# Third block's up product by Strassen's scheme (Winograd's form) over 1024 tokens

## The chip, the cores and the metric

One core of one Trainium2 chip runs the whole program. The metric is device time in microseconds (us); lower is better. The kernel is written instruction by instruction: each engine (PE the matmul engine, ACT, DVE and POOL the elementwise engines, SP the issuer of DMAs) runs its own list in order and meets the others by semaphores only.

## The reference, cut to what matters

`x` has 32 blocks of 128 tokens of 512 features, float32. Two transformer blocks run one after the other; the kernel computes them in three stages, A (attention with 16 heads and layer norm), B (attention with one head over each block of 128 tokens) and C (the MLP of the second transformer block). The change concerns C and what feeds it:

```python
h = film(rmsnorm(x, norm2_w), cond, film2_w, film2_b)      # (32, 128, 512)
h = jax.nn.gelu(h @ mlp_w1 + mlp_b1, approximate=False) @ mlp_w2 + mlp_b2
return x_in + h                                            # w1 512 x 2048, w2 2048 x 512
```

`h @ mlp_w1` is called the up product, the one with `mlp_w2` the down product.

## The kernel before, in words

Every float32 operand of a large product is split in a high half, rounded to fp32r, and a low half, the difference; a product of two such operands takes three matmuls (high with high, high with low, low with high), `split_product`, lines 625 to 627. The 32 blocks are worked in NG = 8 groups of 4 blocks (512 tokens).

Stage B (`body_b(g, first, last)` of every engine, unrolled over g = 0 to 7): PE does four projections of the group's input (`h_g`, m = 0 to 3), then for each block b values (`values_b`), scores, the transpose of the exponentials (`transpose_pb`, L984) and the product with the values (`attend_b`). The last block's transpose and product of a group come after `h_g` 0 and 1 of the next group. Beside it ACT, DVE and POOL prepare the next group: ACT squares and sums the rows (`squares_b`, L1196), DVE makes mean plus epsilon (L1560), POOL raises to the power -1/2 (L1920) and scales the block (`norm_b`, L1923), PE transposes it (L937), ACT applies scale and shift (`scale_b`, L1133) and rounds (L1257), DVE subtracts (L1368). On ACT, `squares_b(g+1, 2)` and `squares_b(g+1, 3)` stand ahead of the first `next_h` of group g, and so ahead of its first exponential (L1308). `xb` has two slots: SP issues a load of it (L486) when the block two earlier has been scaled by POOL. In B the weights of the MLP's first layer are also loaded, rounded by ACT and made low by DVE, one eighth for each group (`split_w1`, L1284), and stay in SBUF.

Stage C (`body_c(g, first, last)`, groups 1 to 6 in a loop of the hardware): PE runs 16 tiles f of 128 hidden features. `up(g, f)` is 12 matmuls of 128 x 512 into bank f % 2; ACT takes the gelu from that bank (L1345), DVE rounds and subtracts (L1847, L1368), and `down(g, f)` follows LAG = 3 tiles later with 12 matmuls into banks 2 to 5. Norms of the next group are spread between the tiles; its transposes (L1055) come near the group's end. DVE adds the residual from the banks (L1859), POOL having added the bias to it (L1905), and SP stores.

The order of everything is written out by hand; there is no planner.

## Time and profile before

| what | value |
|---|---|
| time, median of 3 runs | 1519.54 us (1518.88 to 1519.66) |
| profiled execution's own time | 1519.62 us |
| its span | 1517.8 us |
| PE busy | 1508.4 us (99%), 8904 matmuls |
| DVE / ACT / POOL busy | 826.9 / 588.5 / 586.8 us |
| granted TensorE clock | 1.0 |
| DMA | 125.28 MB, mean 83 GB/s |

The span is from the first to the last instruction of the profiled execution; what lies between it and that execution's time is start and end. PE is busy from end to end, the other engines about half of the time. Stage C begins at about 804.5 us of the span.

### The profile page before, as it was taken

How to read it: one execution, taken by the hardware profiler on the slowest of the kernel's cores; microseconds unless marked ns; L12 is line 12 of the kernel's file. 1: busy time of each engine (PE TensorE's matmuls, PEld its weight loads, DVE VectorE, ACT ScalarE, POOL GpSimd, SP SyncE). 2: the span in 40 equal slices, each digit the busy share in tenths (PEclk: the TensorE clock that was granted, in tenths of full speed). 3: DMA queues.
4: the chain of work that ended last, by engine and by line, in shares of the span. 5: the costliest groups of instructions: out<-in, count | busy, mean ns of one | idle time of the engine just before them, and what ended most of it. 6: DMA issues, size and time to landing. Idle time of an engine off the chain costs nothing.

```text
span 1517.8 us, 24576 instructions
## 1 busy us (share of the span) xinstructions
PE 1508.4 (99%) x8904; PEld 1231.2 (81%) x8904; DVE 826.9 (54%) x1723; ACT 588.5 (39%) x1877; POOL 586.8 (39%) x506
## 2 busy tenths in 40 slices
PE   8999999999999999999999999999999999999999
PEld 5888888888887668888888888888888888888887
DVE  6777777877866676677766242332425233242522
ACT  4655565655544445655554221211212122121210
POOL 6757666676645545545552212030211202121100
PEclk9999999999999999999999999999999999999999
DMA  7222222222126236544444020010201001020100
GB/s 252 67 97 72 90 86 80 96 74 94 56 85 214 93 126 201 165 150 161 152 126 150 31 70 15 33 51 0 76 7 69 14 27 56 0 76 7 56 0 28
DMA packets 64350, 125.28 MB, mean 83 GB/s; under 512 B 6848, under 2 KB 10944, under 8 KB 64256
## 3 DMA queue, kind: packets, MB, share of 16 engines
q1 hardware_dynamic: 63584, 123.95, 24.3%
q8 instruction: 55, 0.90, 0.2%
q14 instruction: 39, 0.32, 0.1%
q10 hardware_dynamic: 672, 0.10, 0.0%
HBM read 98.67 MB, written 25.36 MB: 82 GB/s over the span
## 4 chain that ended last, share of the span: by engine, by line
PE 97%; POOL 1%; DVE 1%; DMA 0%; issue 0%; SPq 0%; ACT 0%
PE bank L625 27%; PE bank L627 27%; PE bank L626 27%; PE bank L716 4%; PE bank L709 2%; PE bank L727 2%; PE bank L1030 2%; PE bank L937 1%; PE bank L766 1%; PE bank L758 1%; PE bank L1055 1%; PE bank L640 1%; POOL xa L1888 1%; DMA wgb<-wb_t_in 0%; POOL rstd L1885 0%; PE bank L650 0%
## 5 line engine op out<-in xcount | busy, mean ns | idle before, releaser
L1847 DVE CAST g_hi<-gf 128x512 fp32r<-128x512 f32 x128 | 68.7, 537 | 427.9 <-ACT gf L1345 427.9
L1345 ACT ACTIVATE gf<-bank,cols 128x512 f32<-128x512 f32 x128 | 88.3, 690 | 513.5 <-PE bank L627 513.5
L1170 ACT ACTIVATE pa<-bank,neg_max 128x128 f32<-128x128 f32 x512 | 181.7, 409 | 136.2 <-DVE neg_max L1463 136.2
L625 PE MATMUL bank<-w_hi,g_hi 128*128 128x512 f32 x512 | 200.5, 392 | 0.0
L627 PE MATMUL bank<-w_hi,g_lo 128*128 128x512 f32 x512 | 199.4, 389 | 0.0
L625 PE MATMUL bank<-hb_hi,w_hi 128*128 128x512 f32 x512 | 199.3, 389 | 0.0
L626 PE MATMUL bank<-w_lo,g_hi 128*128 128x512 f32 x512 | 199.2, 389 | 0.0
L627 PE MATMUL bank<-hb_hi,w_lo 128*128 128x512 f32 x512 | 199.2, 389 | 0.0
L626 PE MATMUL bank<-hb_lo,w_hi 128*128 128x512 f32 x512 | 199.2, 389 | 0.0
L1905 POOL TENSOR_TENSOR xrc<-xrc,b 128x512 f32<-128x512 f32 x32 | 48.3, 1539 | 301.9 <-DMA xrc<-x_dram 301.9
L1933 POOL TENSOR_TENSOR pa<-pa,rec 128x512 f32<-128x512 f32 x128 | 143.0, 1126 | 54.4 <-DVE rec L1486 54.0
L1920 POOL TENSOR_TENSOR rstd<-ve,neg_half 128x1 f32<-128x1 f32 x64 | 44.9, 702 | 282.8 <-DVE ve L1560 282.8
L1170 ACT ACTIVATION_READ_ACCUMULATOR pa<-bank,neg_max 128x1 f32 x512 | 127.1, 248 | 0.0
L627 PEld LDWEIGHTS bank<-w_hi,g_lo 128*128 128x128 f32 x512 | 96.1, 188 | 20.1
L625 PEld LDWEIGHTS bank<-hb_hi,w_hi 128*128 128x128 f32 x512 | 96.1, 188 | 20.1
L627 PEld LDWEIGHTS bank<-hb_hi,w_lo 128*128 128x128 f32 x512 | 96.1, 188 | 20.0
L626 PEld LDWEIGHTS bank<-hb_lo,w_hi 128*128 128x128 f32 x512 | 96.1, 188 | 19.9
L626 PEld LDWEIGHTS bank<-w_lo,g_hi 128*128 128x128 f32 x512 | 96.2, 188 | 19.5
L625 PEld LDWEIGHTS bank<-w_hi,g_hi 128*128 128x128 f32 x512 | 96.1, 188 | 19.5
L1463 DVE TENSOR_REDUCE neg_max<-bank 128x4 f32<-128x512 f32 x128 | 83.3, 676 | 44.3 <-PE bank L709 44.3
L1923 POOL TENSOR_SCALAR xnb<-xb,rstd 128x512 f32<-128x512 f32 x60 | 98.3, 1639 | 10.5 <-POOL rstd L1920 5.3
L1368 DVE TENSOR_TENSOR g_lo<-gf,g_hi 128x512 fp32r<-128x512 f32 x128 | 96.4, 753 | 4.4
(223 smaller groups left out, 3154.8 us busy)
## 6 DMA issues: line engine op xcount, KB each, us to landing
rows<-st_dram SPq DMA_DIRECT2D x32, 512.0 KB, 4.6
xb<-x_dram SPq DMA_DIRECT2D x60, 256.0 KB, 2.8
xa<-xt_in SPq DMA_DIRECT2D x32, 256.0 KB, 4.0
xra<-xt_in SPq DMA_DIRECT2D x32, 256.0 KB, 2.8
x_dram<-h SPq DMA_DIRECT2D x32, 256.0 KB, 2.0
xrb<-x_dram SPq DMA_DIRECT2D x32, 256.0 KB, 2.9
stage_w<-w_in SPq DMA_DIRECT2D x16, 512.0 KB, 3.8
x_dram<-xrb SPq DMA_DIRECT2D x32, 256.0 KB, 2.1
```

The lines of the kernel that those rows point to most:

```text
L625: nc.tensor.matmul(dst, w_hi, a_hi, start=start, stop=False)
L626: nc.tensor.matmul(dst, w_hi, a_lo, start=False, stop=False)
L627: return nc.tensor.matmul(dst, w_lo, a_hi, start=False, stop=stop)
L716: last = nc.tensor.transpose(scores_bank[j][:, m * P:(m + 1) * P], pa[:, j, m, :], ident[:])
L1170: last = nc.scalar.activation(pa[:, j, m, :], scores_bank[j][:, m * P:(m + 1) * P], ACT.Exp, bias=neg_max[:, j * C + m:j * C + m + 1], acc ...
L1345: nc.scalar.activation(gf[f % 2][:], bank[f % 2][:], ACT.Gelu, bias=cols[:, B1_COL + f:B1_COL + f + 1])\
L1368: return nc.vector.tensor_tensor(dst, whole, high.bitcast(F32), ALU.subtract)
L1463: nc.vector.tensor_reduce(neg_max[:, j * C:(j + 1) * C], scores_bank[j][:].rearrange("p (h k) -> p h k", h=C), AX.X, ALU.max, negate=True) ...
L1847: nc.vector.tensor_copy(g_hi[:, r, :], gf[f % 2][:]).then_inc(g_hi_ready, 1)
L1905: nc.gpsimd.tensor_tensor(x[:, i], x[:, i], row[:], ALU.add).then_inc(ready, 1)
L1923: nc.gpsimd.tensor_scalar(xn[:, slot], x[:, i], rstd1[:, i:i + 1], None, ALU.mult).then_inc(ready, 1)
L1933: nc.gpsimd.tensor_tensor(pa[:, j], pa[:, j], rec[:, j * C:(j + 1) * C].unsqueeze(2).broadcast_to([P, C, P]), ALU.mult)\
```

## The change: what it does

The up product is worked for 1024 tokens at a time (s = 0 to 3, two groups each), and as blocks of two by two: W1's 512 input features in two halves, hidden features in two halves of 1024 (tile p of the first half is paired with tile p + 8), tokens in two halves of 512. Each of the NP = 8 pairs of tiles needs seven products of 6 matmuls in place of eight. The products' operands are four blocks of W1 (three of them used directly) with four sums S1 to S4, and of the activations B11, B21, B22 with four sums T1, T2, T3, N4.

- W1's sums are made in B by POOL (`sums_w1`, `low_sums`), rounded by ACT; all seven operands with both halves, 14336 bytes a partition (1792 KB) for each pair, are stored to DRAM (`store_w1`), and in C read back for every pair of every s into a ring of two slots (`load_ring`).
- The products fall in four banks (two products in two of them are added to another one's bank). ACT copies two partial results out, DVE makes five additions with the banks (`add_up`), and ACT takes the four gelus from SBUF.
- Half 0 (512 tokens) is used for the down product at once, two tiles after each pair. The gelus of half 1 go to DRAM (`store_hid`) and come back (`load_hid`, four slots) for 16 tiles of the down product behind the last pair.
- The sums of the activations: for s = 0 in groups 5 to 7 of B (`squares_late`, `norm_late`, `scale_late`, `t3_late`, `rest_first`), for the others during half 1 of C (`combos` on POOL, `round_c` on ACT, `low_c` on DVE). They share SBUF with ring slot 1. Up and down banks change roles with each s.
- C is unrolled, with no loop.

```diff
+PRODUCTS = [(A11, B11, 0, True), (A12, B21, 1, True), (S2, T2, 0, False), (S1, T1, 2, True), (S3, T3, 3, True),
+            (S4, B22, 2, False), (A22, N4, 3, False)]
+NORM_AFTER = (1, 3, 6, 9)
...
 SP body_b
+                if g < NP // 2:
+                    load_w1(2 * g)
+                    load_w1(2 * g + 1)
+                elif g == NP // 2 + 1:
+                    load_late()
...
+                if 1 <= g <= NP // 2:
+                    store_w1(2 * g - 2)
+                    store_w1(2 * g - 1)
...
 SP body_c
+                for p in range(NP):
+                    n = NP * s + p
...
+                    if p < NP - 2 or p == NP - 2 and not last:
+                        sp.wait_ge(up_done, 7 * (n + 1))
+                        load_ring(n + 2)
...
+                    store_hid(n, 1)
+                    store_hid(n, 0)
+                if not last:
+                    load_cx(8 * s)
+                    load_cx(8 * s + 1)
+                for k in range(GB):
+                    load_hid(s, k)
+                if not last:
+                    for j in range(2, 6):
+                        load_cx(8 * s + j)
                 for b in range(GB):
+                    store_y(8 * s + b)
+                load_hid(s, 4)
+                load_hid(s, 5)
+                for b in range(GB):
+                    load_cxr(8 * s + GB + b)
+                for k in range(6, 9):
+                    load_hid(s, k)
                 if not last:
+                    load_cx(8 * s + 6)
+                    load_cx(8 * s + 7)
+                for k in range(9, FT):
+                    load_hid(s, k)
                 if not last:
+                    sp.wait_ge(op_lo_made, 2 * GB + GB * (s + 1))
+                    load_ring(NP * s + NP + 1)
...
 PE up_product(s, p, i): waits of i for p > 0, then 6 matmuls
+                elif i == 0:
+                    pe.wait_ge(up_copied, 2 * n)
+                elif i == 1:
+                    pe.wait_ge(up_summed, 5 * n - 4)
+                elif i == 3:
+                    pe.wait_ge(up_summed, 5 * n - 1)
+                elif i == 4:
+                    pe.wait_ge(up_summed, 5 * n)
+                if i == 0:
+                    pe.wait_ge(ring_in[p % 2], RING_IN + 16 * (n // 2 + 1))
+                elif i == 2:
+                    pe.wait_ge(up_copied, 2 * n + 1)
+                elif i == 5:
+                    pe.wait_ge(up_summed, 5 * n + 2)
+                elif i == 6:
+                    pe.wait_ge(up_summed, 5 * n + 3)
...
 PE body_c
+                for p in range(NP):
+                    for i in range(7):
+                        up_product(s, p, i)
...
+                    if p > 0:
+                        down(s, 0, 2 * p - 2)
+                        down(s, 0, 2 * p - 1)
+                down(s, 0, FT - 2)
+                down(s, 0, FT - 1)
+                for k in range(FT):
+                    down(s, 1, k)
+                    if not last and k in NORM_AFTER:
+                        i = NORM_AFTER.index(k)
+                        norm_c(s, 2 * i)
+                        norm_c(s, 2 * i + 1)
...
 ACT body_b, in the loop over b and behind it
+                    if g == NG - 2:
+                        scale_late(b)
+                        if b > 0:
+                            round_late(b - 1)
+                    if last:
+                        round_first(b)
                 if not last:
                     squares_b(g + 2, 0)
                     squares_b(g + 2, 1)
+                if g == NP // 2 + 1:
+                    squares_late()
...
 DVE body_b, end
+                    if last and b > 0:
+                        low_first(b - 1)
+                if g == NP // 2 + 1:
+                    dve.wait_ge(cssq, GB)
+                    nc.vector.tensor_scalar(ve4[:], ssq4[:], 1.0 / D, EPS_RMS, ALU.mult, ALU.add).then_inc(cvar, 1)
                 dve.wait_ge(brec, GB * g + GB - 1)
                 residual_b(g, GB - 2)
+                if last:
+                    low_first(GB - 1)
...
 DVE add_up(n, i)
+                up, copied, summed = ((2, 1, 0), (4, 2, 0), (5, 0, 2), (6, 2, 0), (7, 2, 0))[i]
+                r = banks(n // NP)[0][(1, 2, 3, 2, 3)[i]]
+                dst, src = ((sum11, p1), (u2p5, u2), (sum22, u2p5), (sum12, u2), (sum21, u2))[i]
+                dve.wait_ge(up_done, 7 * n + up)
...
+                nc.vector.tensor_tensor(dst[:], bank[r][:], src[:], ALU.add).then_inc(up_summed, 1)
...
 DVE body_c, behind the pairs
                 if not last:
+                    mean_square_c(8 * s)
+                    mean_square_c(8 * s + 1)
+                split_hid(s, 0)
+                if not last:
+                    mean_square_c(8 * s + 2)
+                    mean_square_c(8 * s + 3)
+                split_hid(s, 1)
                 for b in range(GB):
+                    residual_c(8 * s + b)
+                split_hid(s, 2, 3)
...
+                    mean_square_c(8 * s + 4)
+                    mean_square_c(8 * s + 5)
+                    split_hid(s, 4)
+                    scale_c(s, 0)
+                    split_hid(s, 5, 6)
+                    low_c(s, 0)
+                    split_hid(s, 7)
+                    scale_c(s, 1)
+                    mean_square_c(8 * s + 6)
+                    mean_square_c(8 * s + 7)
+                    split_hid(s, 8, 9)
+                    low_c(s, 1)
...
+                    scale_c(s, 3)
+                    split_hid(s, 14, 15)
+                    low_c(s, 3)
...
 POOL body_b, end
+                if 1 <= g <= NP // 2:
+                    low_sums(2 * g - 2)
+                    low_sums(2 * g - 1)
+                if g < NP // 2:
+                    sums_w1(2 * g)
+                    sums_w1(2 * g + 1)
+                if g == NP // 2 + 1:
+                    norm_late()
...
+                if last:
+                    for b in range(GB):
+                        rest_first(b)
...
 POOL rest_first(b), combos(s, i)
+                then(combine(t1, h_late[:, 0:2, own], hb_new[:, 0:2, own]))
+                then(combine(t2, h_late[:, 2:C, own], t1))
+                combine(n4, hb_new[:, 2:C, own], t2).then_inc(t_made, 1)
...
+                combine(part[:, T3], part[:, B22], part[:, N4])
+                then(combine(part[:, T1], part[:, N4], part[:, B11]))
+                then(combine(part[:, T2], part[:, B22], part[:, T1]))
+                combine(part[:, N4], part[:, B21], part[:, T2]).then_inc(t_made, 1)
...
 POOL body_c
+                    for j in range(GB):
+                        norm_c(8 * s + j)
+                    combos(s, 0)
+                    norm_c(8 * s + 4)
+                    norm_c(8 * s + 5)
+                    combos(s, 1)
+                    norm_c(8 * s + 6)
+                    norm_c(8 * s + 7)
+                    combos(s, 2)
+                    combos(s, 3)
```

`combine` is a POOL subtraction of 128 x 256 elements; `then` makes POOL wait for it. `load_cx(q)` for q > 1 waits until POOL has scaled the block two before (`xc` has two slots). `norm_c` on PE waits, for the first four blocks, for the four residual additions of half 0, whose banks it writes. `squares_late` squares four blocks that `load_late` fetched; `norm_late` is one power of 128 x 4 and four scalings of 128 x 512.

## Rows read from the trace of the kernel before

**Rows 1.** The page: busy time, share and instructions of each engine.
```profile
PE 1508.4 (99%) x8904; PEld 1231.2 (81%) x8904; DVE 826.9 (54%) x1723; ACT 588.5 (39%) x1877; POOL 586.8 (39%) x506
```

**Rows 2.** The page: the chain that ended last, by engine.
```profile
PE 97%; POOL 1%; DVE 1%; DMA 0%; issue 0%; SPq 0%; ACT 0%
```

**Rows 3.** Stages of C and start: PE, PEld, DVE, ACT, POOL busy; clock, DMA share, GB/s.
```profile
16.00:20.00 4.00, 2.69 (x10) 1.07 (x8) 3.93 (x9) 3.94 (x10) 2.09 (x3) 1.00 1.03 373
...
892.50:980.00 87.50, 87.50 (x396) 72.60 (x395) 29.20 (x54) 17.77 (x34) 14.60 (x13) 1.00 0.11 37
```

**Rows 4.** PE in order of time, C: start, duration, instruction; 24 matmuls between.
```profile
905.06 0.39 PE L625 MATMUL bank<-w_hi,g_hi 128*128 128x512 f32 x1
...
910.50 0.39 PE L625 MATMUL bank<-w_hi,g_hi 128*128 128x512 f32 x1
```

**Rows 5.** Groups by line, whole trace: busy us, mean ns; idle before.
```profile
L625 PE MATMUL bank<-hb_hi,w_hi 128*128 128x512 f32 x512 | 199.3, 389 | 0.0
...
L1272 ACT ACTIVATE vb_hi<-bank 128x512 fp32r<-128x512 f32 x32 | 18.5, 579 | 0.0
L1257 ACT ACTIVATE hb_hi<-hb_new 128x512 fp32r<-128x512 f32 x36 | 22.4, 636 | 9.5 <-PE bank L627 8.1
L1284 ACT ACTIVATE w_hi<-stage_w 128x1024 fp32r<-128x1024 f32 x8 | 8.4, 1044 | 0.0
L1933 POOL TENSOR_TENSOR pa<-pa,rec 128x512 f32<-128x512 f32 x128 | 143.0, 1126 | 54.4 <-DVE rec L1486 54.0
L1920 POOL TENSOR_TENSOR rstd<-ve,neg_half 128x1 f32<-128x1 f32 x64 | 44.9, 702 | 282.8 <-DVE ve L1560 282.8
L1923 POOL TENSOR_SCALAR xnb<-xb,rstd 128x512 f32<-128x512 f32 x60 | 98.3, 1639 | 10.5 <-POOL rstd L1920 5.3 <-issue 4.7 <-ACT hb_hi L1257 0.2
```

**Rows 6.** The same view, C alone, 840 to 1517.8 us.
```profile
L1859 DVE TENSOR_TENSOR xrc<-bank,xrc 128x512 f32<-128x512 f32 x32 | 21.9, 692 | 10.5 <-PE bank L627 10.5
...
L1368 DVE TENSOR_TENSOR w_lo<-stage_w,w_hi 128x1024 fp32r<-128x1024 f32 x2 | 2.4, 1220 | 1.9 <-ACT w_hi L1341 1.9
```

**Rows 7.** ACT, PE and POOL in order of time, groups 5 to 6 of B.
```profile
744.89 0.63 ACT L1196 ACTIVATE junk<-xb 128x512 bf16<-128x512 f32 x1
...
748.95 0.39 PE L625 MATMUL bank<-vb_hi,ptb_hi 128*128 128x512 f32 x1
...
751.22 1.99 POOL L1923 TENSOR_SCALAR xnb<-xb,rstd 128x512 f32<-128x512 f32 x1 [0.17 <-POOL rstd L1920]
...
756.13 0.63 ACT L1196 ACTIVATE junk<-xb 128x512 bf16<-128x512 f32 x1 [2.19 <-issue]
...
762.36 0.27 PE L984 MATMUL bank<-ident,pb 128*128 128x128 f32 x1
```

**Rows 8.** POOL and PE in order of time, group 7 of B and C's start.
```profile
792.76 2.52 POOL L1905 TENSOR_TENSOR xrb<-xrb,cb 128x512 f32<-128x512 f32 x2
...
797.84 0.27 PE L984 MATMUL bank<-ident,pb 128*128 128x128 f32 x1
...
807.24 0.27 PE L984 MATMUL bank<-ident,pb 128*128 128x128 f32 x1
```

**Rows 9.** DMA issues by name: count, KB each, median us to landing.
```profile
xb<-x_dram SPq DMA_DIRECT2D x60, 256.0 KB, 2.8
...
film_w<-film_in SPq DMA_DIRECT2D x2, 2048.0 KB, 10.0
```

**Rows 10.** DVE and POOL in order of time, beside POOL's four bias additions.
```profile
898.03 0.43 DVE L1847 CAST g_hi<-gf 128x512 fp32r<-128x512 f32 x1 [2.96 <-ACT gf L1345]
898.50 0.69 DVE L1368 TENSOR_TENSOR g_lo<-gf,g_hi 128x512 fp32r<-128x512 f32 x1
...
899.05 5.67 POOL L1905 TENSOR_TENSOR xrc<-xrc,b 128x512 f32<-128x512 f32 x4 [40.28 <-DMA xrc<-x_dram]
...
900.63 1.24 DVE L1847 CAST g_hi<-gf 128x512 fp32r<-128x512 f32 x1 [1.44 <-ACT gf L1345]
901.90 1.66 DVE L1368 TENSOR_TENSOR g_lo<-gf,g_hi 128x512 fp32r<-128x512 f32 x1
```

More of the change, by code:

```diff
@@ L41, in wait @@
     engine.wait_ge(sem, value)
-def wait_apart(engine, sem, value, passed):
-    wait(engine, sem, value)
-    if not isinstance(value, int):
-        engine.sem_inc(passed, 1)
 def uses_h(g, m):
@@ L939, in norm_b, with norm_late @@
                 last.then_inc(nb_full, 1)
+            def norm_late(b):
+                pe.wait_ge(cxn, b + 1)
+                pe.wait_ge(nb_free_act, GB * (NG - 2) + b + 3)
+                for c in range(C):
+                    last = nc.tensor.transpose(bank[4 + b % 2][:, c * P:(c + 1) * P], x_late[:, b, c * P:(c + 1) * P],
+                                               ident[:])
+                last.then_inc(ct_full, 1)
             def h_g(g, m, first):
@@ L1116, in _ @@
+            for s in range(NS):
+                body_c(s, s == 0, s == NS - 1)
         @block.scalar
@@ new lines, in squares_late, with scale_late @@
+            def squares_late():
+                act.wait_ge(late_in, 16 * GB)
+                for b in range(GB):
+                    act.wait_ge(bssq, GB * (NG - 1) + 2)
+                    last = nc.scalar.activation(junk[:], x_late[:, b], ACT.Square, accum_out=ssq4[:, b:b + 1])
+                    last.then_inc(cssq, 1)
+                    act.wait_ge(cssq, b + 1)
+            def scale_late(b):
+                act.wait_ge(st_made, 4)
+                act.wait_ge(ct_full, b + 1)
+                affine(bank[4 + b % 2], h_late[:, :, b * P:(b + 1) * P], st_f2[:, GB + b], ct_free_act)
@@ new lines, in body_c @@
+            def body_c(s, first, last):
+                for p in range(NP):
+                    n = NP * s + p
+                    copy_up(n, 0)
+                    if first:
+                        split_w2(p)
+                    copy_up(n, 1)
+                    gelu(n, sum11, 1, 0)
+                    gelu(n, sum22, 3, 1)
+                    gelu(n, sum12, 4, 0)
+                    gelu(n, sum21, 5, 1)
+                if not last:
+                    for j in range(6):
+                        squares_c(8 * s + j)
+                    scale_c(s, 0)
+                    round_c(s, 0)
+                    scale_c(s, 1)
+                    squares_c(8 * s + 6)
+                    squares_c(8 * s + 7)
+                    round_c(s, 1)
+                    for i in range(2, GB):
+                        scale_c(s, i)
+                        round_c(s, i)
@@ L1356, in _ @@
+            for s in range(NS):
+                body_c(s, s == 0, s == NS - 1)
         @block.vector
@@ L1864, in _ @@
+            for s in range(NS):
+                body_c(s, s == 0, s == NS - 1)
+            for b in range(GB):
+                residual_c(NB - GB + b)
         @block.gpsimd
@@ L2003 @@
+            for s in range(NS):
+                body_c(s, s == 0, s == NS - 1)
 def kernel(**inputs):
```

645 lines of the change are left out of this document (429 added, 216 removed).

## The prediction, made before the changed kernel was run

> **What bounds the kernel now.** I read the page's busy times first: PE is busy 99% of the span, DVE 54%, ACT and POOL 39% [rows 1]. The chain of waits says the same, 97% PE [rows 2]. So only two things count: how many matmuls there are, and every instant in which a changed wait holds PE, since PE has no slack in which to hide one. In stage C, 24 matmuls of 128x512 start in 910.50 - 905.06 = 5.44 us, 0.2267 us each [rows 4]; the 0.39 us of the groups by line is how long one is in flight, not its share of the time. A quiet stretch of C has PE at 87.5 of 87.5 us, DVE at 29.2, ACT 17.8, POOL 14.6 [rows 3]: there is room beside PE, but the change spends it.
>
> **The matmuls.** The up product has 512 x 3 = 1536 matmuls [rows 5]. After it has 4 x 8 pairs x 7 products x 6 = 1344. The 192 that go are 192 x 0.2267 = 43.5 us. Down product (1536) and transposes (28 blocks in C or at B's end, as before) keep their number. The profiled execution took 1519.6, as the median of the runs (1519.5), so the sum with all waits hidden is 1519.6 - 43.5 = 1476.1 us.
>
> **The pairs.** Time from a pair's first matmul: products end at 1.36, 2.72, 4.08, 5.44, 6.80, 8.16, 9.52, each 0.16 later in the bank (0.39 less 0.227). ACT's copy (0.58, as L1272 from a bank [rows 5]) of the first runs 1.5 to 2.1; the third product needs it at 2.72. DVE's additions take 0.69 (as L1859 [rows 6]): u2p5 is done by 6.3 and needed at 6.80; sum22 runs 7.0 to 7.7 and is needed at 8.16. Slack 0.4 us or more each, and the down tiles' 5.44 us between pairs lets ACT and DVE finish. I take 0; were each pair to miss by 0.2, 6 us, which is my bound. A ring load is 1792 KB; by the 2048 KB rows it lands in 9 or 10 us [rows 9], and it has 15 at least, except that in pair 0 (no down tiles behind it) the store of the half-1 gelus queues behind a ring load and frees its buffer some 9 us later, at 18.6, where 16.6 is needed: 0 to 2 us for each of 4 s. I take 1 in all, since a load without traffic beside it should be quicker than these rows; bound 8.
>
> **Stage B, groups 1 to 4 (W1's sums).** POOL gets 8 small combinations and two of 1024 a group, ACT 3 us, DVE 1.2, DMA 3.6 MB of stores. POOL's own price for 128x256 has no row: between 0.55 (half of 1.13 at 512) and 0.70 plus a start, from a 128x1 power [rows 5]; I take 0.8. That is some 11 us in a wait of about 11 us that POOL has before the next norm, whose result has 2 us of slack again. I take 0, bound 6.
>
> **Groups 5 to 6 (the late blocks).** Here I expect the first real stall. ACT ends the squares of (7,1) at 745.5 [rows 7]; `squares_late` adds four of 0.74 (0.63 and its read), to 748.6. DVE stands in wait for them, ahead of a residual addition, the copy of projection 0 and the transposed exponentials: these are ready at 751.0, and PE wants them at 748.95 [rows 7]: 2.0 us. POOL then starts `norm_late`: a power (0.9) and four scalings of 1.58, to 756.3, and only then the norms of (7,0) and (7,1), done at 761.4 where the row ends at 753.2. The load of (7,3) waits for the latter, and landed 2.9 us behind it (756.13); now 764.3. ACT does its squares ahead of `next_h(6,0)` and the exponential: 0.74 + 2.8 + 0.4, so that the transpose of 762.36 [rows 7] comes at 768.3. Together 6.0 us. Group 6 has 2.3 us more ACT work for each block (6 us for four scales, 3.4 for the roundings) beside 4.9 + 0.4 us of PE: 0.7 us at its end.
>
> **Group 7 and C's start.** `round_first(0)` stands on ACT ahead of exponential 1 and waits for POOL, which ends its additions at 795.3 [rows 8]; three combinations and two waits, 2.7, give 798.0, rounding 768 elements 0.84 (between 0.64 and 1.04 [rows 5]), exponential 0.37: 799.2, wanted at 797.84 [rows 8]: 1.4 us. The same happens to the last block: `rest_first(3)`, `round_first(3)`, `low_first(3)` (1.0) follow one another, and since DVE has `low_first(3)` ahead of the copy of the transposed exponentials, block 3's transpose is 1.4 late and its product 2.8 more. Sum 5.6. Stage B and C's start: 6.0 + 0.7 + 5.6 = 12 us; bounds 4 (the late norms slip in somewhere) and 20.
>
> **Half 1 of s = 0, 1, 2.** T is the start of pair 7. PE leaves half 0 at T + 9.5 + 4 x 2.72 = 20.4, then takes 2.72 a tile. DVE is free at 12.6. Blocks 0 and 1 of the next s are fetched behind the last `store_hid` (11.1); with 2.8 to landing [rows 9], squares, POOL's power and scaling (0.7 + 0.2 + 1.6 [rows 5]) they are scaled at 17.8 and 20.2. Their slots free, blocks 2 and 3 land at 20.7 and 23.0, and `mean_square_c` of block 3 stands on DVE ahead of `split_hid(1)`: 23.9 + 1.2 = 25.1, wanted at 23.1: 2.0 us. Then four residuals (2.8) stand ahead of tile 2: 0.6. Later tiles 8 and 9 stand behind the mean squares of blocks 6 and 7, whose loads wait for POOL's norms 4 and 5, which wait for `combos` 0 (4 x 0.8 + 0.3): 1.5 us. From there to the end four rounds of `scale_c`, `combos` (3.5), `round_c` (1.7 for 1792 elements, by ACT's slope of 0.8 ns each) and `low_c` (2.0, by DVE's 1.22 at 1024 [rows 6]) with splits between run some 9 us a round: the last ends near T + 73, and PE wants tile 13 at 63 and the next s at 71: 2.9 us, at tiles 13 and 14 and at the seam. Sum 7 us a seam, 21 for three. The last s has no norms, no stall.
>
> **A row that speaks against it.** A split takes DVE 0.43 + 0.69; beside POOL's additions 1.24 + 1.66, 1.8 us more [rows 10]. POOL, at a sixth of the time in C before [rows 3], works about 27 of the 46 us of half 1 now. At 0.3 us more a split I get 7 us a seam (used above), with 0.9 nearly 13, with none 4. The Trainium skill (GPSIMD Engine Reference, Specifications) says that POOL's SBUF interfaces are shared with VectorE, with contention for DVE instructions in a 2-port mode or with two SBUF inputs; both instructions of a split are of these kinds, and the trace agrees. By it every split beside POOL is slow, which is the second rival.
>
> **Sum.** 1519.6 - 43.5 + 12 (B) + 21 (seams) + 1 (stores) = 1510.1. I forecast **1510 us**. In a 4 us stretch with PE busy 2.69 us the clock stayed granted at 1.00 [rows 3], so stalls of 2 to 4 us should not cost clock.
>
> **Rivals.**
> First, the waits are covered better than I reckon: B costs 4, a seam 2 to 4. For it: many of my stalls are below 2 us, built from landings of 2.8 us that can be 2.0. Against: the orders on ACT, DVE and POOL are fixed, and the 6 us of group 5 need no fine number. 1519.6 - 43.5 + 4 + 9 + 1 = 1490 (1480 to 1500).
> Second, the other side: DVE is the bound of half 1, because POOL holds it up. Half 1 has 16 splits (18.4 us), residuals 2.8, scales 5.5, low halves 8, in all 35 of 46 us. With 1.4 more a split and POOL's own operations at 0.9, the chain of rounds ends 20 us late: 1519.6 - 43.5 + 20 (B, where the same meets `low_sums`) + 60 + 4 = 1560; it is slower than before from 10.5 us a seam on, with B at 12. For it rows 10, and that DVE cannot start early; against, that DVE works from the banks a third of the time, and that additions there took 0.69.
> Third, DMA: stores of 3.6 MB a group in B, or ring loads at 15 us each, hold up the loads of blocks and gelus. Before, C used 0.11 of DMA [rows 3]; now about 120 GB/s of ring and 30 of the rest, where 373 GB/s were had at a full share [rows 3]. 8 us for pair 0 and 6 in B more than above: 1522, no change or slower.
>
> **Chances.** Forecast (1500 to 1519) 0.45, first rival 0.31, second 0.16, third 0.08. Below 0.2% (3 us) a measurement can't tell a change: 1516.5 to 1522.6. Faster 0.76, same 0.07, slower 0.17. The range, from the bounds (B 4 and seams at 4 below; seams at 13 above): 1489 to 1529.
>
> **What will show it.** PE matmuls 8712 in number; 42 matmuls a pair without a wait in the pairs. PE idle near the first transpose of group 6, about 4 us, released by ACT, and 2 us before at the product of group 5's last block. PE idle on g_lo at tile 1 of half 1, with DVE waiting for squares of `xc`. POOL waiting little in half 1, and DVE's splits beside it longer. Wrong would be: waits on the ring or on sums inside pairs, or no idle time at the seams.

## The result: 1536.7 us, slower than before

The changed kernel took 1536.72 us (median of 4 runs, 1533.75 to 1544.06) against 1519.44 for the kernel before (1518.88 to 1519.66): ratio 1.0121, 95% interval 1.0086 to 1.0157. Forecast was 1510 (1489 to 1529), faster. The four runs lie 10 us apart (mean granted clocks 0.989 to 0.997), so what one edit gains against this kernel is known to some 5 us. The profiled execution took 1537.3 us with a span of 1535.5. The working stands beside [rows 1, 2]: the page's first row, and the chain of waits by engine.

```profile
PE 1482.2 (97%) x8712; PEld 1199.4 (78%) x8712; DVE 927.8 (60%) x1862; ACT 653.8 (43%) x1975; POOL 690.2 (45%) x600
...
PE 78%; DMA 6%; POOL 6%; DVE 5%; issue 3%; ACT 2%; SPq 0%; DVEq 0%; POOLq 0%; ACTq 0%
```

The 192 matmuls are gone, and every other engine has more to do. PE's share of the chain fell from 97 to 78%: followed back, a fifth of the span now leads through other engines, though PE itself is busy for 97% of it. PE's waits, grouped (who waited, for whom, us in total, times, longest):

```profile
PE bank L1210 <- DVE sum L2126: 10.5, 4, 3.3
PE bank L714 <- DVE g_lo L1615: 8.1, 7, 2.1
PE bank L1167 <- POOL xnc L2422: 7.0, 3, 2.5
PE bank L1086 <- ACT pb L1501: 6.4, 4, 3.1
PE bank L714 <- DVE ptb_lo L1615: 6.3, 4, 2.2
PE bank L1210 <- DVE op_lo L1615: 2.4, 2, 1.2
PE bank L1030 <- ACT h_late L1281: 1.9, 2, 1.1
...
PE bank L1030 <- POOL xnb L2282: 1.5, 1, 1.5
```

These eight rows are what the change added: 44.1 us in 27 waits, where the forecast had 34. They sit in three places: 10.5 in the pairs (first row), 17.5 in half 1 of s = 0, 1, 2, which is called a seam here (`g_lo`, `xnc`, `op_lo`), and 16.1 in stage B and at C's start (`pb`, `ptb_lo`, `h_late`, `xnb`). But 1476.1 + 44.1 is 1520, not 1537.3. The other 17 us are not in these rows; most of them lie behind the waits. PE around one of them, in order of time (start, duration, instruction, idle before):

```profile
848.05 0.39 PE L1214 MATMUL bank<-op_hi,ring 128*128 128x512 f32 x1
851.28 0.50 PE L1210 MATMUL bank<-op_hi,ring 128*128 128x512 f32 x1 [2.84 <-DVE sum L2126]
851.62 0.40 PE L1212 MATMUL bank<-op_lo,ring 128*128 128x512 f32 x1
...
852.91 0.63 PE L714 MATMUL bank<-w_hi,g_hi 128*128 128x512 f32 x1
853.33 0.63 PE L715 MATMUL bank<-w_lo,g_hi 128*128 128x512 f32 x1
853.76 0.63 PE L716 MATMUL bank<-w_hi,g_lo 128*128 128x512 f32 x1
```

Two costs are to be seen. First, the starts on either side of the wait are 3.23 us apart and the next one follows after 0.34. With 0.227 for each, as in [rows 4], these two steps would take 0.45, so the wait costs 3.12, not the 2.84 shown: 0.28 more. (The idle time is counted from the end of a matmul in flight, 0.16 late, and the first step behind it takes 0.11 longer.) For 27 waits, 7.6 us. Second, from 852.91 the matmuls stand 0.427 us apart: 512 columns at 1.2 GHz, the lower of TensorE's two levels. Windows around four waits (PE, PEld, DVE, ACT, POOL busy; granted clock; DMA share; GB/s):

```profile
816.00:824.00 8.00, 5.97 (x26) 5.30 (x27) 4.19 (x10) 6.18 (x16) 5.45 (x7) 0.79 0.06 22
...
848.00:856.00 8.00, 5.16 (x16) 3.74 (x16) 4.13 (x7) 2.17 (x3) 0.00 (x0) 0.79 0.65 219
...
984.00:992.00 8.00, 6.21 (x20) 5.03 (x21) 7.51 (x14) 3.30 (x7) 6.29 (x4) 0.79 0.47 132
...
1028.00:1036.00 8.00, 4.74 (x21) 3.72 (x21) 4.13 (x7) 2.18 (x3) 0.00 (x0) 1.00 0.33 94
```

0.79 over 8 us is 1.7 us lost, three times here; the wait of 3.26 us at 1031.49, in the last row, brought no fall. The same 0.79 stands at 772 to 780 and at 1336 to 1344, so there were five falls, 8.5 us in all. (The mean clock of 0.994, a rounded figure, gives (1 - 0.994) x 1535.5 = 9.2 us, between 8.4 and 10.0.) The Trainium skill (TensorE: Matmul & The Clock Gate, HAM oscillation) describes a kernel whose every wait for data, longer ones than any here, sends PE back to half rate; in this trace five of 27 waits, of 2.1 to 3.1 us, had such a stretch behind them, and others as long had none.

The sum: 1476.1 + 44.1 + 7.6 + 8.5 = 1536.3, where 1537.3 was measured; 1 us stays unexplained.

### The profile page after: what moved, and what is told of

Same layout as the page of the kernel before. It is cut to its first block, busy times and chain, and to the rows that moved or that the text cites. A ratio compares the mean times of both kernels' runs of the same rounds, so it can differ in the third digit from the quotient of the medians.

```text
span 1535.5 us, 24236 instructions
## 1 busy us (share of the span) xinstructions
PE 1482.2 (97%) x8712; PEld 1199.4 (78%) x8712; DVE 927.8 (60%) x1862; ACT 653.8 (43%) x1975; POOL 690.2 (45%) x600
## 4 chain that ended last, share of the span: by engine, by line
PE 78%; DMA 6%; POOL 6%; DVE 5%; issue 3%; ACT 2%; SPq 0%; DVEq 0%; POOLq 0%; ACTq 0%
PE bank L714 16%; PE bank L716 15%; PE bank L715 15%; PE bank L1210 5%; PE bank L1214 5%; PE bank L1212 5%; PE bank L805 4%; DMA hid_dram<-sum 2%; PE bank L798 2%; PE bank L816 2%; DMA xc<-x_dram 2%; POOL combo L2326 1%; POOL xnc L2422 1%; PE bank L1132 1%; PE bank L855 1%
## 5 line engine op out<-in xcount | busy, mean ns | idle before, releaser
L1210 PE MATMUL bank<-op_hi,ring 128*128 128x512 f32 x448 | 175.3, 391 | 13.0 <-DVE sum L2126 10.5
L1214 PE MATMUL bank<-op_hi,ring 128*128 128x512 f32 x448 | 174.5, 390 | 0.0
L1212 PE MATMUL bank<-op_lo,ring 128*128 128x512 f32 x448 | 174.3, 389 | 0.0
L1566 ACT ACTIVATE sum<-sum,cols 128x512 f32<-128x512 f32 x128 | 92.5, 722 | 122.7 <-DVE sum L2126 122.4
L2264 POOL TENSOR_TENSOR xrc<-xrc,b 128x512 f32<-128x512 f32 x32 | 47.9, 1529 | 209.5 <-DMA xrc<-x_dram 209.5
L2418 POOL TENSOR_TENSOR rstd<-ve,neg_half 128x1 f32<-128x1 f32 x24 | 18.8, 784 | 249.9 <-DVE ve L2090 249.7
L1210 PEld LDWEIGHTS bank<-op_hi,ring 128*128 128x128 f32 x448 | 84.1, 188 | 33.3 <-DVE sum L2126 12.2
L2264 POOL TENSOR_TENSOR xra<-xra,bp 128x512 f32<-128x512 f32 x32 | 48.4, 1513 | 127.7 <-DMA xra<-xt_in 127.7
L2126 DVE TENSOR_TENSOR sum<-bank,p 128x512 f32<-128x512 f32 x32 | 22.1, 690 | 134.5 <-PE bank L1214 134.2
L1214 PEld LDWEIGHTS bank<-op_hi,ring 128*128 128x128 f32 x448 | 84.1, 188 | 17.6
L1212 PEld LDWEIGHTS bank<-op_lo,ring 128*128 128x128 f32 x448 | 84.1, 188 | 17.2
L1728 DVE COPY pta<-bank 128x512 f32<-128x512 f32 x128 | 79.5, 683 | 28.7 <-PE bank L805 28.6
```

Source lines behind the costliest of these rows:

```text
L1210: nc.tensor.matmul(dst[:], part[:, w, 0, c, :], op_hi[:, a, c, :], start=opens and c == 0, stop=False, skip_group_check=True)
L1212: nc.tensor.matmul(dst[:], part[:, w, 0, c, :], op_lo[:, a, c, :], start=False, stop=False, skip_group_check=True)
L1214: last = nc.tensor.matmul(dst[:], part[:, w, 1, c, :], op_hi[:, a, c, :], start=False, stop=c == 1, skip_group_check=True)
L1566: nc.scalar.activation(dst[:], dst[:], ACT.Gelu, bias=cols[:, B1_COL + f:B1_COL + f + 1])\
L1728: nc.vector.tensor_copy(pta[:, j].rearrange("p m q -> p (m q)"), scores_bank[j][:]).then_inc(pt_copied, 1)
L2264: nc.gpsimd.tensor_tensor(x[:, i], x[:, i], row[:], ALU.add).then_inc(ready, 1)
```

## The experiments

Each kernel is the changed kernel with the edit shown, unless it says otherwise. The kernel before, run beside them on the same chip, took 1519.3 to 1519.5 us.

**1. The gelu stores ahead of the ring load.** SP's queue in C:

```
+                    store_hid(n, 1)
+                    store_hid(n, 0)
                     if p < NP - 2 or p == NP - 2 and not last:
                         sp.wait_ge(up_done, 7 * (n + 1))
                         load_ring(n + 2)
...
-                    store_hid(n, 1)
-                    store_hid(n, 0)
```

> In every pair the stores of half 1's gelus are issued ahead of the next ring load. Theory A (the store queues behind a 1792 KB ring load, so its buffer comes free late): DVE's wait on the store in pair 1 of each s (15.5 us in 4) goes, PE's waits there (10.5 us, and about 0.3 us restart each) go with it, and the stretch of half clock after the first of them (1.7 us): 12 to 14 us less, 1523 to 1525 against 1537. Rival B (DMA as a whole is too loaded, the order does not matter): the store still lands after 8 us and PE waits as before; 1537.

1522.42 us, ratio 1.0024 (1.0014 to 1.0033): 14.3 us less. All four waits on `sum` are gone. The cause in the changed kernel, on DVE, and DMA issues of the changed kernel (KB each, median us to landing):

```profile
850.53 0.69 DVE L2126 TENSOR_TENSOR sum<-bank,u2p 128x512 f32<-128x512 f32 x1 [4.09 <-DMA hid_dram<-sum]
```

```profile
ring<-w_dram SPq DMA_DIRECT2D x32, 1792.0 KB, 8.4
...
hid_dram<-sum SPq DMA_DIRECT2D x64, 256.0 KB, 8.6
```

and the same two rows of this kernel:

```profile
ring<-w_dram SPq DMA_DIRECT2D x32, 1792.0 KB, 7.5
...
hid_dram<-sum SPq DMA_DIRECT2D x64, 256.0 KB, 2.3
```

A store of 256 KB issued 0.5 us behind a load of 1792 KB on the same queue took 8.6 us, and 2.3 ahead of it. In the changed kernel the ring load was issued at 840.57 and the store at 841.04; the second half's sum, which overwrites the stored buffer, could start at 850.53. Theory A holds. Not all of the 14.3 us are this wait's: in this kernel's trace 30.1 us of added waits in 22 are left, 14.0 less than before the edit; two waits in groups 1 to 4, which this edit does not touch, are among those that are absent (more on them at the fifth). The four waits alone come to 10.5 + 4 x 0.28 = 11.6 us, with 1.7 more for the fall of the clock behind the first of them.

**2. The late blocks one group earlier.**

```
-                elif g == NP // 2 + 1:
+                elif g == NP // 2:
                     load_late()
...
+                if g == NP // 2 + 1:
+                    squares_late()
                 squares_b(g + 1, 2)
```

with ve4, which waits for these squares on DVE, moved up behind the third `mean_square`.

> The four late blocks of the next stage are loaded in group 4, squared at group 5's start, so that POOL scales them in its idle time of group 5 and not ahead of the norms of group 7. Theory A (POOL held up by norm_late delays the norms, by them the loads, squares and the exponentials): the three waits of 1.7, 1.5 and 3.1 us at groups 5 to 6 go, with restarts 0.9 and half clock 3: 7 to 10 us less, 1527 to 1530. Rival B (ACT's added scales in group 6 are the bound and take over the wait): only 2 to 3 us less, the transposes of group 6 still wait for ACT.

1528.98 us, ratio 1.0056 (1.0037 to 1.0074): 7.7 less, theory A. In the changed kernel, ACT, DVE and POOL show the step as the forecast had it:

```profile
750.68 0.63 ACT L1451 ACTIVATE junk<-x_late 128x512 bf16<-128x512 f32 x1
...
753.70 0.17 DVE L2072 TENSOR_SCALAR ve<-ssq 128x4 f32<-128x4 f32 x1 [3.71 <-ACT junk L1451]
...
753.95 1.04 POOL L2351 TENSOR_TENSOR rstd<-ve,neg_half 128x4 f32<-128x4 f32 x1 [11.81 <-DVE ve L2072]
755.09 6.20 POOL L2354 TENSOR_SCALAR x_late<-x_late,rstd 128x512 f32<-128x512 f32 x4
```

Four squares, then 7.2 us of POOL with the next norms behind them. PE's waits there, 1.74, 1.53 and 3.12 us, are gone in this kernel; of its waits between 740 and 790 us only 2.1 us on `h_late` are left.

**3. Group 7: each rounding after the next exponential.**

```
-                    if last:
-                        round_first(b)
+                    if last and b > 0:
+                        round_first(b - 1)
```

with `round_first(3)` at the group's end, and `low_first(3)` behind the copy of the transposed exponentials.

> In group 7 ACT rounds the sums of block b - 1 behind exponential b and the next block's work, and DVE copies the last transposed exponentials ahead of the last low half. Theory A (round_first stands ahead of the exponential, low_first ahead of the copy): waits of 2.4, 0.6 and 2.2 us at the end of B go, with restarts 0.9 and half clock 1.7: 5 to 7 us less, 1530 to 1532. Rival B (POOL's rest_first itself is too late for the third product): the wait moves to the third up product and less than 2 us is won.

1536.26 us (1532.65 to 1539.09): 0.5 less, nothing that can be told from no change. The waits were 2.39, 0.57 and 2.21 us and became 0.60, 1.19 and 1.36, so three waits of 3.2 us in all took the place of three of 5.2: `low_first(b - 1)` on DVE now waited for the rounding that had been put later (1.21 us at 819.57). Rival B's size came true, not its cause. The first pair's wait behind them is 4.74 us here and 2.84 in the changed kernel, but it is 4.4 in the second experiment and 4.5 in the fourth, which leave group 7 alone, so this growth is not the edit's.

**4. Half 1: splits, loads and transposes in another order.**

```
-NORM_AFTER = (1, 3, 6, 9)
+NORM_AFTER = (1, 3, 8, 11)
...
                 split_hid(s, 0)
+                split_hid(s, 1)
                 if not last:
...
+                    split_hid(s, 8, 9)
                     mean_square_c(8 * s + 6)
```

> At the seams: the split of gelu tile 1 ahead of the mean squares of blocks 2 and 3, those of tiles 8 and 9 ahead of blocks 6 and 7, gelu load 9 ahead of these blocks' loads, and PE's transposes of blocks 4 to 7 two tiles later. Theory A (PE waits for orders written too tightly, DVE itself has idle time): waits at tile 1 (3.8 us in 3), at the transposes (7.0 in 3) and at tile 8 (3.9 in 2 and a part) go, the end of the round chain stays (about 1.5 us a seam, or grows to 3): 10 to 14 us less in all, 1523 to 1527. Rival B (POOL holds DVE up through the port they share, so that half 1 is bound by DVE's and POOL's work): the waits come back at tiles 10 to 15 and at the next s; under 4 us won.

1536.48 us (1534.0 to 1538.37), 0.2 less. The waits at tile 1, at the transposes and at tile 8 went, and four others stand at 980.52, 990.86, 1001.20 and 1010.87: 10.3, 10.3 and 9.7 us apart, the length of one round (scaling, combinations, rounding and low half of one block). What sets that length, on DVE and POOL in the changed kernel:

```profile
991.54 3.94 POOL L2326 TENSOR_TENSOR combo<-combo 128x256 f32<-128x256 f32 x4 [1.54 <-DVE combo L2102]
...
997.25 2.02 DVE L1615 TENSOR_TENSOR op_lo<-combo,op_hi 128x1792 fp32r<-128x1792 f32 x1 [2.37 <-ACT op_hi L1548]
...
1001.77 3.95 POOL L2326 TENSOR_TENSOR combo<-combo 128x256 f32<-128x256 f32 x4 [6.28 <-DVE combo L2102]
```

POOL stands 6.28 us for DVE's scaling while DVE stands 2.37 for ACT's rounding: neither is the bound, the row from one to the other is. Rival B's sign came true (the waits came back, under 4 us won), its cause, work on DVE and POOL as the bound, did not.

**5. W1's low sums on POOL in four pieces.**

```
-                combine(w1_parts[:, r, S1:S4 + 1, 1], w1_sums[:, r], w1_parts[:, r, S1:S4 + 1, 0].bitcast(F32))\
-                    .then_inc(w1_sums_low, 1)
+                for v in range(4):
+                    last = combine(w1_parts[:, r, S1 + v, 1], w1_sums[:, r, v],
+                                   w1_parts[:, r, S1 + v, 0].bitcast(F32))
+                last.then_inc(w1_sums_low, 1)
```

> One edit to the changed kernel: in groups 1 to 4 of stage B, POOL's addition of 128x1024 for the low halves of W1's sums is done in four additions of 128x256. Theory A: the long addition (2.38 us) holds DVE's split of hb beside it (2.97 us where 0.69 is usual), and DVE late is PE's wait before the attend product (1.35 us at 622.33, 1.03 at 685.26, .54 elsewhere). With pieces of 0.7 us DVE's split gets in between: it takes under 1.6 us, those waits go, and the time falls by 2.5 to 4 us with their restarts. Theory B: DVE loses the same time in slices, since POOL works as long or longer in all (8 x 0.73 = 5.8 us for 4.76): the splits stay at 2 to 3 us, no gain, -1 to +2 us.

1539.33 us (1536.27 to 1542.94); its interval overlaps the changed kernel's. The contention is real: POOL and DVE in the changed kernel,

```profile
615.18 4.76 POOL L2326 TENSOR_TENSOR w_parts<-w_sums,w_parts 128x1024 fp32r<-128x1024 f32 x2
...
617.52 2.97 DVE L1615 TENSOR_TENSOR hb_lo<-hb_new,hb_hi 128x512 fp32r<-128x512 f32 x1
```

and in this one:

```profile
615.82 6.02 POOL L2326 TENSOR_TENSOR w_parts<-w_sums,w_parts 128x256 fp32r<-128x256 f32 x8
...
617.87 1.30 DVE L1615 TENSOR_TENSOR hb_lo<-hb_new,hb_hi 128x512 fp32r<-128x512 f32 x1
```

A subtraction of 0.69 us took 2.97: it ended at 620.49, 0.55 behind POOL's second addition. The Trainium skill (SBUF — State Buffer, SBUF: two separate sides) says that a VectorE operation with two SBUF inputs and a GpSimd one that reads SBUF lock the shared ports for a whole instruction, so that the later one "fully blocks"; this row agrees. With short pieces it took 1.30, and the two waits on `ptb_lo` behind it (1.35 us at 622.33, 1.03 at 685.26) are not in this trace. But they are not in that of the first experiment's kernel either, where POOL's additions are as the change has them:

```profile
614.58 5.26 POOL L2326 TENSOR_TENSOR w_parts<-w_sums,w_parts 128x1024 fp32r<-128x1024 f32 x2
616.89 0.68 DVE L1615 TENSOR_TENSOR hb_lo<-hb_new,hb_hi 128x512 fp32r<-128x512 f32 x1
```

There DVE's subtraction came 2.31 us behind the start of POOL's additions, 0.03 us sooner than in the changed kernel (2.34), got in ahead of the second one and took 0.68. With POOL's additions unedited, waits on `ptb_lo` in groups 1 to 4 come to 2.4 us in the changed kernel, 2.6 in the third and fourth, 1.5 in the second, and none in the first, sixth, eighth, ninth and tenth. So that long additions block DVE is shown, that the pieces took these waits away is not, and the time did not fall. A gain of 3 us can't be excluded.

**6. The rounds of half 1 overlapped.** Besides moves like those of the fourth (`NORM_AFTER` is (1, 3, 7, 10), so the transposes come one tile later, not two): DVE scales block i + 1 ahead of the low half of block i, ACT likewise.

```
                     split_hid(s, 4)
                     scale_c(s, 0)
-                    split_hid(s, 5, 6)
+                    split_hid(s, 5)
+                    scale_c(s, 1)
+                    split_hid(s, 6)
                     low_c(s, 0)
```

> The same move of the norms and splits in half 1 as in the run with the seam's order changed, and besides the rounds are overlapped: DVE does the scaling of block i+1 ahead of the low half of block i, and ACT the scaling of block 1, 2, 3 ahead of the rounding of the block before, so that POOL's combinations of the next block run beside the rounding and the low half of this one. Theory A: what holds PE at the seams is the length of a round, scale (1.4) to combinations (4.0) to rounding (1.7) to low half (2.0) to split, 10.2 us in a row for three tiles of 2.72 each (8.2). Overlapped, a round is bounded by its costliest engine, POOL with 4 to 6 us; the waits on op_lo and g_lo in half 1 (17.5 us in three seams with 16 restarts) go for the most part: -12 to -20 us against the changed kernel. Theory B: DVE's own work beside POOL is the bound: then nothing is gained by overlapping, since DVE still does the same: 0 to -4 us. Theory C: the wait of 2.5 us before the transposes of the next s (POOL's fourth or fifth norm) is by itself and stays: -8 to -12.

1548.64 us, ratio 1.019 (1.0175 to 1.0206): 12 slower, which no theory had. g_lo's waits went from 8.1 us in 7 to 20.8 in 17. Those on `xnc` and `op_lo` went, so all added waits are 46.1 us in 32, only 2.0 us more than the changed kernel's; the lower mean clock (0.990 against 0.994) makes some 6 of the 12 us. A miss from my order: DVE and POOL in this kernel,

```profile
984.90 0.15 DVE L2091 TENSOR_SCALAR ve<-ssq 128x1 f32<-128x1 f32 x1 [3.63 <-ACT junk L1528]
```

```profile
971.38 3.62 POOL L2328 TENSOR_TENSOR combo<-combo 128x256 f32<-128x256 f32 x4 [9.21 <-DVE combo L2103]
```

DVE stood 3.63 us for block 7's squares, whose load waits for norm 5, which stands on POOL behind combinations that had themselves waited 9.21 us for a scaling. All the rest then fell together with POOL's additions of rows.

**7. All of these together** (group 7 with four buffers of `t_first` in place of two, so that low halves come two blocks later).

> All edits together: the gelu store ahead of the ring load (-14 by its own run), the late blocks a group earlier (-8 by its own run), W1's sums in four pieces, the rounds of half 1 overlapped with the changed order at the seams, and in group 7 the rounding of block b after exponential b+1 with its low half one block later still, for which t_first gets a fourth buffer. Theory A, the losses are separate waits of PE and add up: 1536.7 - 14.3 - 7.7 - 3 - 16 - 6 = 1490 (1482 to 1500); clock granted above 0.997. Theory B, the same engines' work returns as waits elsewhere, as in the two reorderings before: 1505 to 1515, no better than what the store and the late blocks give together.

1519.21 us, ratio 0.9998 (0.9989 to 1.0007). Worse than either theory, and its waits tell why. Those in the pairs and those of the late blocks are gone, one of 1.5 us stands in group 5 (734.95), group 7 has 2.8 us left (of 5.2), and `g_lo` has 21.8 us in 21 waits: the sixth's seams, which the next run takes out.

**8. Stores, late blocks and group 7 alone.** Half 1 and the sums as the change has them.

> The changed kernel with three edits together: the gelu store ahead of the ring load, the late blocks a group earlier, and in group 7 the rounding of block b after exponential b+1 with its low half one block later still (t_first with four buffers). Half 1 and W1's sums stay as the change has them. Theory A, losses ahead of C, at the pairs and at the seams are separate: 1536.7 - 14.3 - 7.7 = 1514.7, less 4 to 6 for group 7 (5.2 us of waits there, of which 3 remained in the combined run): 1508 to 1513, faster than before by 0.4 to 0.8%. Theory B, the combined run's 1519 was not the seams' fault and the edits overlap: 1517 to 1521.

1512.76 us (1508.78 to 1513.25), ratio 0.9951 (0.9938 to 0.9965): faster than before, theory A. So the fifth and sixth edits cost 6.4 us of the combined kernel. The accounts close here too: 21 added waits of 25.3 us in all, 21 x 0.28 = 5.9, granted clock 1.00: 1476.1 + 25.3 + 5.9 = 1507.3, where this execution took 1509.0.

**9. Half 1 planned anew, on top of the eighth.** POOL: norm 4, combinations 0, norm 5, combinations 1; loads of blocks 6 and 7 behind them; `NORM_AFTER = (1, 3, 5, 8)`; each scaling right behind its transposes:

```
                     mean_square_c(8 * s + 4)
+                    scale_c(s, 0)
                     mean_square_c(8 * s + 5)
                     split_hid(s, 4)
-                    scale_c(s, 0)
-                    split_hid(s, 5, 6)
+                    mean_square_c(8 * s + 6)
+                    split_hid(s, 5)
+                    scale_c(s, 1)
                     low_c(s, 0)
```

> The kernel of the run before this one, and half 1 planned anew: norm 4 ahead of combinations 0 and norm 5 ahead of combinations 1 on POOL, blocks 6 and 7 loaded behind them, the scalings of a round right behind its transposes, the transposes after tiles 1, 3, 5 and 8, each low half a split later. In the overlapped run DVE stood 3.6 us for the squares of block 7 and POOL 9.2 us for the first scaling, and the last three rounds then met POOL's additions of rows, with splits of 2.1 to 3.1 us where 1.1 is usual. Theory A, this was a question of order: the rounds end by tile 12, seam waits fall from 17.5 to under 6 us for three, and the time is 12 to 18 us below the run beside it: 1492 to 1500. Theory B, DVE and POOL together have too much to do in half 1, whatever the order (POOL some 47 us of 46, DVE some 38 with each split beside POOL 0.3 longer): g_lo waits of 10 us or more remain, gain under 6 us.

1513.32 us (1508.94 to 1513.64): no gain on the eighth, theory B's number. `g_lo` kept 15.5 us in 14 waits, with one of 2.2 us late in each seam and behind it a second, of 1.0 in the first and 2.2 in the other two. What stands there, on DVE and POOL of this kernel:

```profile
973.74 7.86 POOL L2270 TENSOR_TENSOR xrc<-xrc,b 128x512 f32<-128x512 f32 x4
```

```profile
974.25 1.50 DVE L2143 CAST g_hi<-hid 128x512 fp32r<-128x512 f32 x1
975.78 1.65 DVE L1620 TENSOR_TENSOR g_lo<-hid,g_hi 128x512 fp32r<-128x512 f32 x1
977.35 3.10 DVE L1620 TENSOR_TENSOR op_lo<-combo,op_hi 128x1792 fp32r<-128x1792 f32 x1
```

The rounds were over early, and so POOL's four additions, which had stood at the seam's end, came forward onto the last splits and low half.

**10. Those additions later.** The ninth and one wait on POOL:

```
                     combos(s, 3)
+                    pool.wait_ge(g_lo_ready, 2 * FT * s + FT + 14)
                 add_rows(s, 1)
```

> The kernel of the newly planned half 1 with one more edit: POOL starts its four additions of 128x512 rows of half 1 only when DVE has done 14 of the 16 splits. In its trace these additions (7.86 us for four, 973.7 to 981.6) stand beside two splits, 1.50 and 1.65 us for cast and subtraction where 0.42 and 0.69 are usual, and a low half of 3.10 us where 2.0 is usual; PE then waits 2.2 us twice in each seam, and the granted clock is 0.79 in an 8-us window behind them. Theory A, contention between POOL's additions and DVE is what is left of the seams: the two waits of 2.2 us a seam go, g_lo waits fall from 15.5 to under 6 us, clock above 0.998, the time falls by 8 to 14 us to 1500 to 1505. Theory B, DVE's own order is the limit there (a low half of 2 us between splits that PE wants every 2.72): the waits shrink by less than 1 us each and come back at tile 14 or at the residuals, gain under 4 us.

1506.46 us (1503.39 to 1509.31), ratio 0.9911 (0.9897 to 0.9925): 6.9 below the ninth and the fastest of all, 0.9% under the kernel before. The low half takes 2.02 us and the splits beside it 1.1 again; the second of the two late waits went in each seam, `g_lo` fell to 10.8 us in 10. The additions have not stopped holding DVE up: they now stand on the last splits, where PE has no need of them yet:

```profile
980.85 6.23 POOL L2270 TENSOR_TENSOR xrc<-xrc,b 128x512 f32<-128x512 f32 x4 [4.93 <-DVE g_lo L1620]
981.14 1.67 DVE L1620 TENSOR_TENSOR g_lo<-hid,g_hi 128x512 fp32r<-128x512 f32 x1
```

A's mechanism is shown for the second wait; gain, `g_lo` (under 6 us forecast) and clock (above 0.998 forecast, 0.995 in the profiled execution) all fell short. The other wait, 2.23 us at 976.61, stands beside POOL's combinations, 6.85 us for six at 969.07, but also behind a low half that had waited 1.22 us for ACT's rounding, so what holds it, contention or the order, is not shown.

**11. What a wait costs: eight long ones.** The kernel before, with nothing of the change. In the last group of C, PE waits in every second tile, between its up product and its down product, for four chained ACT operations:

```
+                    if last and f in HOLD:
+                        pe.wait_ge(wk_first, 2 + HOLD_OPS * (HOLD.index(f) + 1))
```

> The kernel before, without the change, and with eight waits of PE put into the down product of the last group of stage C (one ahead of every second tile), each until four operations in a row on ACT, started when PE reaches it at the latest by a counted chain, are done. Theory A, from the changed kernel's trace: a wait of 2 to 3 us costs PE more than the idle time shown: about 0.3 us each to fill its pipe again, and where the clock falls to half for some 3.4 us, 1.7 us more: with eight waits the time grows by the idle shown plus 2.4 us, plus 1.7 for each fall, of which I expect 3 to 6. Theory B: a wait costs its idle time alone, as the prediction took it: the growth of the span is within 1 us of the idle time shown, and the granted clock stays at 1.00.

1560.34 us, ratio 1.0264 (1.0248 to 1.028): 40.8 us for eight waits of 3.28, 26.2 in all. Theory B, idle time alone, is refuted; theory A had 3 to 6 falls of the clock, and in the trace there is one behind each of the eight. Two stretches between waits, with two tiles of 24 matmuls and one wait in each:

```profile
1462.49:1478.58 16.09, 12.80 (x49) 10.08 (x49) 2.24 (x4) 3.79 (x6) 0.00 (x0) 0.86 0.00 0
1478.58:1495.69 17.11, 13.84 (x48) 10.85 (x48) 2.24 (x4) 3.79 (x6) 0.00 (x0) 0.80 0.00 1
```

**12. Eight short ones.** `HOLD_OPS` 2 in place of 4.

> The kernel before with the same eight waits as in the other run on waits, of two ACT operations each in place of four: some 1.7 us for 3.28. The long ones cost 40.8 us in the runs for 26.2 us of idle time, since TensorE's granted clock was 0.80 to 0.89 in the tiles behind them. Theory A, the fall of the clock needs a wait of above 2 us: short ones cost their idle time and 0.2 to 0.4 us each, 16 us in all, clock above 0.998. Theory B, any repeated wait brings the half clock: more than 20 us, clock under 0.995.

1542.95 us, ratio 1.0151 (1.0136 to 1.0167): 23.6 us for 15.7 of idle time (1.96 each). Two stretches of this kernel, and the same two tiles in the kernel before:

```profile
1458.14:1471.27 13.13, 11.17 (x48) 8.93 (x48) 2.24 (x4) 2.53 (x4) 0.00 (x0) 1.00 0.00 0
1471.27:1486.02 14.75, 12.79 (x49) 10.07 (x49) 2.24 (x4) 2.53 (x4) 0.00 (x0) 0.88 0.00 1
```

```profile
1443.39:1454.27 10.88, 10.88 (x49) 9.01 (x49) 2.24 (x4) 1.38 (x2) 0.00 (x0) 1.00 0.00 0
```

At full clock a stretch is 10.88 + 1.96 + 0.29 = 13.13: the fixed price of a wait, apart from its length, is 0.29 us, as at 851.28 above. With a fall of the clock it is 1.62 more (14.75); in the run before this one, 16.09 and 17.11 against 10.88 + 3.28 + 0.29 = 14.45 make 1.6 and 2.7. In the trace of the long waits all six stretches of two tiles are longer than 14.45; of the short ones' stretches of two tiles three are 14.7 and three 13.1. The span grew by 23.7 here, of which 15.7 + 8 x 0.29 + 3 x 1.62 = 22.9 is so accounted for. Theory A's condition, a length above 2 us, is wrong; B's sum (over 20) came true and its clock (under 0.995) did not, at 0.997. What decides whether a wait brings a fall stays open.

## Why the prediction was wrong, step by step

- **The matmuls: right.** 8712 of them, and the cadence of 0.227 holds wherever nothing waits.
- **"Stalls of 2 to 4 us should not cost clock": the step that failed most.** It rested on one 4 us window in the kernel's first 20 us [rows 3], a start with half-filled work, as evidence for waits in a full stream. In the profiled execution stalls of 2.1 to 3.1 us had five falls behind them, 8.5 us; the eleventh and twelfth show it without the change.
- **The price of a wait by itself was missing from the sum.** 27 x 0.28 = 7.6 us. [rows 4] had its first half: 0.39 in flight against a spacing of 0.227 means that any idle time shown is 0.16 short.
- **The pairs: 1 taken, 10.5 measured; bound 8.** Its own sign of being wrong, waits on sums inside pairs, came. The text found the mechanism, the buffer and the hour (store behind ring load, free some 9 us later), then took 1 "since a load without traffic beside it should be quicker than these rows". It was not quicker: 1792 KB in 8.4 us, and [rows 9] had 2048 KB in 10.0, nearly the same rate. A hope took the place of the row.
- **Groups 1 to 4: 0 taken, 2.4 us of idle time.** Here [rows 10], weighed for half 1, was carried back to B in the second rival and in no term of the sum: POOL's longest addition, 2.38 us, holds DVE ahead of two attend products. This term is 0 to 2.6 us in the other kernels, by the hundredths of a microsecond shown at the fifth.
- **Groups 5 and 6: 6.0 forecast, 6.7 measured (1.74, 1.53, 3.12, 0.32), 7.7 less time in the second run.** The end of the squares, DVE's wait and POOL's scalings came in the order given. Group 6's own 0.7 was 1.9 us on `h_late`.
- **Group 7: 5.6 forecast, 5.2 measured.** To mend it took four buffers of `t_first` in place of two; with them, 2.4 us of the 5.2 went.
- **The seams: 21 forecast, 17.5 measured.** Tile 1, the transposes and tile 8 waited, and the row of rounds ended late by 1.2 us. The row itself was reckoned at 9 us a round and takes 10.2 (from 991.54 to 1001.77 above). The extra per split, 0.3, is what was measured: beside work of POOL g_lo 0.859 against 0.692, g_hi 0.556 against 0.433 (means of 15 in half 1, and of 15 in half 0):

```profile
L1615 DVE TENSOR_TENSOR g_lo<-hid,g_hi 128x512 fp32r<-128x512 f32 x15 | 12.9, 859 | 0.5
L1615 DVE TENSOR_TENSOR op_lo<-combo,op_hi 128x1792 fp32r<-128x1792 f32 x4 | 8.7, 2172 | 7.1 <-ACT op_hi L1548 7.1
L2140 DVE CAST g_hi<-hid 128x512 fp32r<-128x512 f32 x15 | 8.3, 556 | 3.4 <-DMA hid<-hid_dram 3.4
```

```profile
L1615 DVE TENSOR_TENSOR g_lo<-sum,g_hi 128x512 fp32r<-128x512 f32 x15 | 10.4, 692 | 0.5
L2140 DVE CAST g_hi<-sum 128x512 fp32r<-128x512 f32 x15 | 6.5, 433 | 6.3 <-ACT sum L1566 6.3
```

- **The rivals.** The first (1490) needed waits better covered; they were not. The second, DVE as the bound, is false for the changed kernel: DVE stands 7.1 us for roundings in that half 1. Its contention decides once the rounds are overlapped (ninth and tenth runs). The third had the right mechanism, the gelu stores, but at 8 us and a chance of 0.08; its terms add up to 1523, not 1522.

So waits were 10 us over the forecast, 9.5 of it in the one term that was set against its own row, and the 17 us that follow waits had no term at all. Without these two the account gives some 1510 us, faster than before; that this is the forecast's number is luck, since the terms for B (4 short) and the seams (3.5 over) cancel. The range failed by its making too: its upper end has only the seams at their bound. With B at 20 and the stores at 8, the text's own bounds, it is 1476.1 + 20 + 39 + 8 = 1543, which holds the 1536.7. (Its lower end, by the terms named, is 1493 and not 1489.)

## What to carry to other kernels

Where one engine is busy 99% of the time, price a wait on it as its length, plus a fixed start (0.28 us here), plus a chance of a clock fall (1.6 us and more here): 27 waits of 1.6 us on average, five of them with a fall, cost some 61 us, not 44. Count the waits, not only their sum; a change that spreads work over four engines pays it at every hand-over, and here paid 61 us for 43.5. On a queue, put the small transfer whose buffer is wanted soon ahead of the large one that has time. And look for a wait in several kernels before an edit is credited with its absence.

## What was not expected of the hardware

- A 256 KB store behind a 1792 KB load on one queue lands after 8.6 us, ahead of it after 2.3.
- Eight waits of 1.96 us lost 23.6 us and eight of 3.28 lost 40.8; the clock stood at 1.2 GHz for 8 matmuls or more (1.6 us at 0.2 each) behind some waits and not behind others of the same length in the same loop.
- Four of POOL's additions, moved from DVE's splits and low half to its last splits, gave 6.9 us with no work taken away, nearly what the late blocks' step was worth (7.7).
- The same DVE subtraction beside the same two POOL additions took 2.97 us when it came 2.34 us behind their start, and 0.68 when it came 2.31 behind.
